# A layer norm's square root moved from all 128 partitions to four: Sqrt and reciprocal of per-token rows instead of Ln and Exp of a whole tile

## The reference

```python
def _layernorm(x, axis=-1, eps=1e-05):
    m = jnp.mean(x, axis=axis, keepdims=True)
    v = jnp.var(x, axis=axis, keepdims=True)
    return (x - m) / jnp.sqrt(v + eps)

x = L0_attn_x
x = x + 0.5 * _L0_ffn_ref(_layernorm(x, axis=-1), ...)     # two layers of local attention + GLU, each with a norm inside
x = x + _L0_attn_ref(_layernorm(x, axis=-1), ...)          # a scan
x = x + 0.5 * _L0_ffn_ref(_layernorm(x, axis=-1), ...)
x = x + 0.5 * _L1_ffn_ref(_layernorm(x, axis=-1), ...)     # spiking FFN
x = x + _L1_attn_ref(_layernorm(x, axis=-1), ...)          # 16 small heads
x = x + 0.5 * _L1_ffn_ref(_layernorm(x, axis=-1), ...)
x = x + 0.5 * _L2_ffn_ref(_layernorm(x, axis=-1), ...)
x = x + _L2_attn_ref(_layernorm(x, axis=-1), ...)
x = x + 0.5 * _L2_ffn_ref(_layernorm(x, axis=-1), ...)
x = x + 0.5 * _L3_ffn_ref(_layernorm(x, axis=-1), ...)     # 16 small heads, then routed experts, a norm before each
x = x + _L3_attn_ref(_layernorm(x, axis=-1), ...)          # a gated scan
x = x + 0.5 * _L3_ffn_ref(_layernorm(x, axis=-1), ...)
```

## Time and profile before

| what | value |
|---|---|
| median of 3 runs (lowest, highest) | 2577.56 us (2577.18, 2582.08) |
| the profiled execution, its own time | 2577.56 us |
| its span, first to last instruction | 2575.8 us |
| TensorE, matmuls | 1936.9 us, 75% |
| VectorE | 1377.8 us, 53% |
| ScalarE | 1184.5 us, 46% |
| GpSimd | 543.0 us, 21% |
| chain that ended last, by engine | PE 59%, DVE 19%, ACT 10%, issue 6% |

### The profile page before, as it was taken

The page is one execution under the profiler, slowest core; times in us unless marked ns, Lnnn a source line. Parts: engine busy times, 40 slices in busy tenths (PEclk is TensorE's granted clock), DMA queues, the critical chain, the costliest instruction groups (busy, mean ns, idle before and its releaser), DMA issues.

```text
span 2575.8 us, 36677 instructions
## 1 busy us (share of the span) xinstructions
PE 1936.9 (75%) x14096; PEld 962.2 (37%) x14096; DVE 1377.8 (53%) x2359; ACT 1184.5 (46%) x2408; POOL 543.0 (21%) x679
## 2 busy tenths in 40 slices
PE   6786877777787777868689964557898855688985
PEld 2444244433244423443234422223344442244434
DVE  4553465433555345543644367753677544467745
ACT  3454344432444425544524453235477724357762
POOL 2331134200333114320032000001322120223202
PEclk9998999988999799988879987688799977679997
DMA  3000000000000000000043000000444120243402
GB/s 138 1 2 1 0 1 1 2 0 0 1 1 1 1 0 1 1 1 1 0 97 60 3 0 0 0 0 20 97 86 88 26 66 0 49 88 79 86 16 82
DMA packets 50148, 70.81 MB, mean 27 GB/s; under 512 B 4980, under 2 KB 37972, under 8 KB 49464
## 3 DMA queue, kind: packets, MB, share of 16 engines
q1 hardware_dynamic: 47416, 60.07, 10.8%
q0 software_dynamic: 2560, 8.39, 1.2%
HBM read 50.59 MB, written 16.88 MB: 26 GB/s over the span
## 4 chain that ended last, share of the span: by engine, by line
PE 59%; DVE 19%; ACT 10%; issue 6%; POOL 4%; DMA 2%; SPq 0%; POOLq 0%; DVEq 0%; ACTq 0%
PE ps L196 56%; DVE arena L1144 3%; DVE arena L562 3%; ACT arena L509 2%; ACT arena L268 2%; ACT arena L270 2%; PE ps L425 2%; POOL arena L664 1%; POOL arena L657 1%; PE ps L1027 1%; DVE arena L635 1%; ACT arena L518 1%; DVE arena L908 1%; DVE arena L910 1%; DMA arena<-scratch 1%
## 5 line engine op out<-in xcount | busy, mean ns | idle before, releaser
L196 PE MATMUL ps<-arena 128*18 128x256 f32 (+10 forms) x10088 | 719.3, 313 | 196.2 <-DVE arena L1144 47.0
L196 PEld LDWEIGHTS ps<-arena 128*18 128x18 f32 (+6 forms) x10088 | 388.5, 127 | 509.8 <-issue 179.9
L1144 DVE TENSOR_REDUCE arena<-ps 128x2 f32<-128x512 f32 (+1 forms) x640 | 396.9, 661 | 239.2 <-PE ps L196 236.5
L196 PE MATMUL ps<-arena,w_L0f 128*128 128x512 f32 (+3 forms) x800 | 345.9, 569 | 95.9 <-DVE arena L573 28.3
L1128 ACT ACTIVATE arena<-ps 128x1024 f32<-128x1024 f32 (+1 forms) x320 | 313.1, 982 | 134.0 <-PE ps L196 129.6
L509 ACT ACTIVATE arena<-ps,arena 128x128 f32<-128x128 f32 x512 | 227.4, 459 | 112.0 <-DVE arena L606 111.9
L196 PE MATMUL ps<-arena,const 128*32 128x512 f32 (+2 forms) x616 | 228.8, 633 | 44.9 <-ACT arena L1467 19.5
L196 PEld LDWEIGHTS ps<-arena,w_L0f 128*128 128x128 f32 (+2 forms) x800 | 148.0, 201 | 257.2 <-issue 155.5
L664 POOL TENSOR_TENSOR arena<-arena 128x512 f32<-128x512 f32 x128 | 133.0, 1039 | 310.6 <-DVE arena L578 310.6
L562 DVE TENSOR_TENSOR arena<-ps,arena 128x1024 f32<-128x1024 f32 x128 | 152.7, 1220 | 66.8 <-PE ps L196 35.3
L518 ACT ACTIVATE arena<-ps 128x512 f32<-128x512 f32 x128 | 76.0, 598 | 226.2 <-PE ps L196 226.2
(11 more groups left out here) (227 smaller groups left out, 2286.7 us busy)
## 6 DMA issues: line engine op xcount, KB each, us to landing
scratch<-arena SPq DMA_DIRECT2D x40, 384.0 KB, 2.8
arena<-scratch SPq DMA_DIRECT2D x80, 192.0 KB
arena<-scratch SPq DMA_DIRECT2D x80, 128.0 KB
arena<-scratch SPq DMA_DIRECT2D x80, 88.0 KB
w_L0f<-in_L0f SPq DMA_DIRECT2D x2, 1557.0 KB, 12.2
arena<-arena SPq DMA_DIRECT2D x80, 12.0 KB
const<-in_const SPq DMA_DIRECT2D x1, 1276.0 KB, 7.6
residual<-in_x SPq DMA_DIRECT2D x1, 1024.0 KB, 5.0
```

The lines of the kernel that those rows point to most:

```text
L196: return self.nc.tensor.matmul(o, lhsT, rhs, start=start, stop=stop, skip_group_check=True)
L1144: V.tensor_reduce(self.mx[k % 2][:, :, at:at + 1], ps[:, i % 2, 0:SEQ + self.n1].rearrange("p (t s) -> p t s", t=self.blocks), AXX, ALU.ma ...
```

## The change

Each token's variance is now kept once instead of 128 times. For chunk c TensorE multiplies `sq` by `meanrow`, in four pieces of 128 tokens, so that row t of a 4x128 block holds the variances of piece t (in bank 2c+1, `k.tilerow` and `meanrow` exist already). ScalarE takes Sqrt of 4x128, VectorE its reciprocal, and TensorE spreads the four rows back to 128 partitions with `tilerow` (into the same bank). As a multiply would otherwise read two banks, ScalarE also copies x - m to the destination right behind the Square, and VectorE multiplies in place. Every step now runs over all four chunks before the next step begins, on each engine. The load at the start of a normalisation is gone.

```diff
 class Norm(Stage):
     def __init__(self, k, src, dst, eps, sq, sd, scale=None, shift=None):
...
-        self.logged, self.inverted = self.sig("logged", NCHUNK), self.sig("inverted", NCHUNK)
+        self.copied = self.sig("copied", NCHUNK)
+        self.rooted, self.inverted, self.spread = self.sig("rooted", NCHUNK), self.sig("inverted", NCHUNK), self.sig("spread", NCHUNK)
...
     def tensor(self, eng, src_ready=None):
         k, ps = self.k, self.k.ps
-        for c in range(NCHUNK + 1):
-            if c < NCHUNK:
-                if src_ready is not None:
-                    src_ready(eng, c)
-                k.mm(ps[:, 2 * c, :], k.K("center"), self.src[:, chunk(c)]).then_inc(self.centered.sem, 1)
-            if c > 0:
-                self.wait_ge(eng, self.squared, c)
-                k.mm(ps[:, 2 * c - 1, :], k.K("mean"), self.sq[:, chunk(c - 1)]).then_inc(self.summed.sem, 1)
+        for c in range(NCHUNK):
+            if src_ready is not None:
+                src_ready(eng, c)
+            k.mm(ps[:, 2 * c, :], k.K("center"), self.src[:, chunk(c)]).then_inc(self.centered.sem, 1)
+        for c in range(NCHUNK):
+            self.wait_ge(eng, self.squared, c + 1)
+            for t in range(4):
+                m = k.mm(ps[0:4, 2 * c + 1, 0:P], k.K("meanrow")[:, 4 * t:4 * t + 4],
+                         self.sq[:, c * CHUNK + t * P:c * CHUNK + (t + 1) * P], start=t == 0, stop=t == 3)
+            m.then_inc(self.summed.sem, 1)
+        for c in range(NCHUNK):
+            self.wait_ge(eng, self.inverted, c + 1)
+            for t in range(4):
+                m = k.mm(ps[:, 2 * c + 1, t * P:(t + 1) * P], k.tilerow[:, t * P:(t + 1) * P], self.sd[0:4, c * P:(c + 1) * P])
+            m.then_inc(self.spread.sem, 1)
 
     def scalar(self, eng):
         k, ps, S = self.k, self.k.ps, self.k.nc.scalar
-        S.preload_act_table_set("natural_log_exp_and_others")
-        for c in range(NCHUNK + 1):
-            if c < NCHUNK:
-                self.wait_ge(eng, self.centered, c + 1)
-                S.activation(self.sq[:, chunk(c)], ps[:, 2 * c, :], ACT.Square).then_inc(self.squared.sem, 1)
-            if c > 0:
-                sd = self.sd[:, chunk(c - 1)]
-                self.wait_ge(eng, self.summed, c)
-                S.activation(sd, ps[:, 2 * c - 1, :], ACT.Ln, bias=k.C(self.eps)).then_inc(self.logged.sem, 1)
-                self.wait_ge(eng, self.logged, c)
-                S.activation(sd, sd, ACT.Exp, scale=-0.5).then_inc(self.inverted.sem, 1)
+        for c in range(NCHUNK):
+            self.wait_ge(eng, self.centered, c + 1)
+            S.activation(self.sq[:, chunk(c)], ps[:, 2 * c, :], ACT.Square).then_inc(self.squared.sem, 1)
+            S.activation(self.dst[:, chunk(c)], ps[:, 2 * c, :], ACT.Copy).then_inc(self.copied.sem, 1)
+        for c in range(NCHUNK):
+            self.wait_ge(eng, self.summed, c + 1)
+            S.activation(self.sd[0:4, c * P:(c + 1) * P], ps[0:4, 2 * c + 1, 0:P], ACT.Sqrt, bias=k.C(self.eps)[0:4, :]).then_inc(self.rooted.sem, 1)
 
     def vector(self, eng, ch):
         k, ps, V = self.k, self.k.ps, self.k.nc.vector
         for c in range(NCHUNK):
-            self.wait_ge(eng, self.inverted, c + 1)
+            self.wait_ge(eng, self.rooted, c + 1)
+            r4 = self.sd[0:4, c * P:(c + 1) * P]
+            V.reciprocal(r4, r4).then_inc(self.inverted.sem, 1)
+        for c in range(NCHUNK):
+            self.wait_ge(eng, self.spread, c + 1)
+            self.wait_ge(eng, self.copied, c + 1)
             d = self.dst[:, chunk(c)]
-            if self.scale is None:
-                h = V.tensor_tensor(d, ps[:, 2 * c, :], self.sd[:, chunk(c)], ALU.mult)
-            else:
-                ch.did(V.scalar_tensor_tensor(d, ps[:, 2 * c, :], k.C(self.scale), self.sd[:, chunk(c)], ALU.mult, ALU.mult))
-                ch.wait_ge()
-                h = V.tensor_scalar(d, d, k.C(self.shift), None, ALU.add)
+            h = V.tensor_tensor(d, d, ps[:, 2 * c + 1, :], ALU.mult)
+            if self.scale is not None:
+                ch.did(h)
+                ch.wait_ge()
+                h = V.tensor_scalar(d, d, k.C(self.scale), k.C(self.shift), ALU.mult, ALU.add)
             h.then_inc(self.done.sem, 1)
```

## The result

| | time |
|---|---|
| before, median of 4 runs (lowest, highest) | 2577.43 us (2577.18, 2582.08) |
| after, median of 4 runs (lowest, highest) | 2661.99 us (2650.30, 2668.25) |
| ratio, 95% interval | 1.0336 (1.0303 to 1.0369) |
| forecast | 2653.5 us, range 2632 to 2690 |

The change makes the kernel 3.4% slower; the forecast had 2.95%. The profiled execution of after took 2663.19 us against 2577.56, 85.6 more. The chain of the new norm was forecast. That the sum came out near is partly luck: a norm that holds the clock costs less than I had (48 to 59 for 76, experiment 5), and a clock that does not hold, which I had left out, costs 27 to 39.

The account below looks back on a forecast made before the run. The prediction took ScalarE, at 1.72 us per chunk, to set the normalisation's pace. Its terms 12.9+8.7+18.3+13.0+10.8+12.2 = 75.9 us, added to 2577.6, gave 2653.5 us, range 2632 to 2690.

Parts of the forecast that it names:

- 76: All 20 normalisations and the stages they delay: the terms together add 75.9 us to the kernel's time.
- ScalarE's 1.72 per chunk: In the old normalisation, Square, Ln and Exp take 1.72 us per chunk, and ScalarE sets the pace.
- The reciprocals: On VectorE, four 4x128 reciprocals per normalisation, all ahead of the first multiply, 0.87 us each back to back.
- The loads: 13 square-root table loads between last Copy and first Sqrt, 1.28 us each; the other 7 normalisations need none.
- Rival 4: Each mid-normalisation load costs a second load length because ScalarE's queue must empty: +17, 2671 us; chance 0.03.
- cold, plain, with load: Normalisation starting at TensorE half clock, unscaled, with a Sqrt table load: last multiply ends at 14.9 us.
- warm, with load: Normalisation with TensorE at 2.4 GHz from the start and a Sqrt table load: ends at 13.05 us.
- two in a row, warm, and cold: Paired normalisations: the second's centring waits behind the first's spreads; ends 24.9 and 28.4 us, 12.2 more together.
- rival 1: Narrow passes of 4 columns or rows leave TensorE at 1.2 GHz, next stage starting at half clock: 2686 us; chance 0.12.
- two wide products of two passes each (4x0.43): Glu's start at chunk 1, at 14.75 us: these products put the first Gelu at 16.8 against 12.03.
- rival 3: TensorE stays awake through the normalisation, so following stages run at 2.4 GHz: 2564 us at 180 us; chance 0.02.
- Rival 2: In seven Glu, Scan and Spike starts, later work takes up the late normalisation: minus 31.3, 2622 us; chance 0.07.

Follow-up runs that it names:

- experiment 5: The changed kernel with the spreading passes over all 128 rows, zeros in the added ones; 2630.08 us, ratio 1.0186 to the kernel before.
- experiment 12: The kernel before with four extra 128-column passes on TensorE ahead of each of the 80 averaging passes; 2636.96 us, ratio 1.0245.
- Experiment 1: The changed kernel with each 4x128 reciprocal run twice on VectorE; 2733.33 us, ratio 1.0618 to the kernel before.
- experiment 3: The changed kernel with Ln and Exp on the four rows replacing Sqrt and reciprocal, their table loaded at the norm's start; 2641.91 us, ratio 1.0277.
- experiment 2: The changed kernel with the Sqrt table loaded at each norm's start instead of between Copy and Sqrt; 2646.19 us, ratio 1.0285.
- experiment 6: The kernel before, unchanged, timed against itself; 2569.19 us, ratio 0.998.
- experiment 10: The changed kernel with Ln and Exp on four rows, table loaded at the start, Copy moved to VectorE, spreading over 128 rows; 2621.07 us, ratio 1.0200.
- experiment 11: The kernel of experiment 10 with the spreading passes taking the four rows alone; 2649.46 us, ratio 1.0318 to the kernel before.
- experiment 9: The kernel of experiment 5 with 7 more Sqrt table loads behind the last Copy, 20 in all; 2626.39 us, ratio 1.0206 to the kernel before.

## Why the prediction was right, and where not

**The bound.** I read ScalarE's 1.72 per chunk as what sets the pace. It was half of the truth: TensorE's work per chunk is as long (experiment 12). That step failed without harm, since I priced the new norm by its own chain, in which TensorE appears.

**The reciprocals: right.** Forecast 0.87 back to back from the row of 0.940: 3.38 for four. It is the 128 along a partition that count. Experiment 1 shows that a further reciprocal lengthens the path; experiment 3, that TensorE's passes stand ready to set the end without them.

**The loads: right.** 13 of them, 0.01 to 0.02 between neighbours. Rival 4 is out: no load costs more than itself (13x1.28 = 16.6, and experiment 2 gave 13 to 16). The Trainium skill ("ScalarE: Activation LUTs", section "What ACT_TABLE_LOAD costs") has about 1380 ns of drain beside the 1283; none of the 13 shows it (17 to 19 ns before, 12 behind).

**The norm's end, from the first centring pass:**

| kind | forecast | measured |
|---|---|---|
| cold, plain, with load | 14.9 | 14.24 (second Spike); 16.25 (first L0Norm), 16.43 (first of the cold pair) |
| cold, no load (first L2Ffn) | 13.9 | 14.07 |
| warm, with load | 13.05 | 12.67 (last L2Ffn); 13.85 (L3Scan) |
| warm, no load | 11.8 | 11.78 (first of the warm pair); 12.65 (L2Attend) |
| scaled, with load | 17.1 | 16.67 |
| first Gelu | 16.8 | 17.61 |
| two in a row, warm, and cold | 24.9, 28.4 | 25.98, 30.96 |

Where a row has more than one value, the later ones are norms in which the clock fell during the spreads and stretched them (32 in 4.71 to 5.20 instead of 3.83); that is part of rival 1's picture, in 5 of 20 norms. In the two plain ones over 16 the centring passes also stayed longer at half clock (6.52 and 6.69, where I had 5.2).

**The terms of the sum**, by stage, against what the stages grew by (from the end of the stage before to their own end):

| stages | forecast | measured |
|---|---|---|
| L0Norm, L1Attend, L2Attend, L3Scan (5) | 12.9 | 11.7 |
| L2Ffn (2) | 8.7 | 8.7 |
| Glu (4) | 18.3 | 23.4 |
| Spike, Scan (3) | 13.0 | 14.2 |
| L3Experts (2) | 10.8 | 7.8 |
| L3Attend with two norms (2) | 12.2 | 12.0 |
| Attend behind L0Norm and Glu (4) | 0 | 7.0 |
| all | 75.9 | 84.9 of 85.6 |

The row of Glu fails most. Its step, "two wide products of two passes each (4x0.43)", takes full clock; these four passes ran from 557.47 to 560.91, 3.44 for 1.72, at half clock. They started 14.17 after the first centring pass where I had 14.75, which is why the first Gelu came only 0.8 late. Within the first row the single stages differ more (first L0Norm 5.1 for 3.4, L3Scan 6.1 for 3.1, L2Attend -2.2 for 1.9); those with Attend in them, the 7.0 of the last row too, are as uncertain as experiment 6 shows.

**Rival 1, held at 0.12, was half right.** "Passes with 4 columns or 4 rows": passes of four columns keep the clock up (in the Glu norm it stands at 1.0 through all sums), those of four rows don't. The clock did not stay low, as the rival had it; it was up and fell. The price I gave it was 32. Measured: 39 by the ratios of experiment 5, with an uncertainty of some 12, 28 in experiments 10 and 11, 27 by the spans of two single executions (2661.4 against 2634.3). **And the forecast's 76 was too high for a norm that holds the clock:** the span of experiment 5 is 58.6 above before, its median 48 by the ratio. Clock held, Glu grows by 4.1 to 4.3 instead of 4.4 to 4.75, the pairs' stages by 1.1 and 3.7 instead of 5.7 and 6.5, probably because the stage behind starts with the clock up: a piece of rival 3 (17 us for it at most, the whole difference). Two errors of opposite sign: by the spans 27 - 17 = 10, which is the 85.6 against the forecast's 75.9. Without the four Attend stages, L1Attend and L2Attend, where up to 6.1 came and went without any change in experiment 6, the picture is the same: forecast 71.9, after 79.5, experiment 5 57.2. So the sum lay in its range by luck as well as by reasoning: the term for the clock was left out, and the terms of the norms were together some 15 us too large.

**Rival 2** (the stage takes up the delay) is out: Glu, Spike and Scan grew by 4.1 to 6.6 each.

**Where the 84 us lie, then.** 27 to 39 are the clock that the four-row passes let fall. The rest, about 48 by experiment 5's ratio, is covered by TensorE's 32 spreading instructions a norm, which have no counterpart in before: as many passes alone cost 61 (experiment 12). Reciprocals, Copy and load lie beside this work and end a little later than it: with the clock held, taking the reciprocals and the middle load away and moving the Copy to VectorE, experiments 9 to 10, gives 5 us, which the intervals don't tell from nothing. What stays open: how the 48 and the 61 go together exactly (the averages of before are also replaced by sums of about the same length), and whether the early load is still worth something once the clock holds.

No kernel here beats the one before; the best with folded rows, experiments 5, 9 and 10, are 1.9 to 2.1% slower, and their intervals don't tell them apart.

## What to carry to other kernels

Before moving work off the engine that seems to set the pace, add up what each other engine does in the same stretch: here ScalarE and TensorE both filled 1.72 per chunk, so relief for ScalarE that was paid for in passes on TensorE could only lose. A cost found by doubling an instruction is what one more costs; what is gained by taking it out has to be tried by itself (71 against 4). And an operand of a few rows makes a pass neither shorter nor harmless: here it took as long as one over 128 rows, and the granted clock fell at it or behind it.

## What the runs showed of the hardware

- At a norm's 32 passes over four rows, or within 1.7 us behind them, the granted clock fell to half in 135 of 140 norms, also where TensorE had been busy for 3.80 of 3.80 us; with the same passes over 128 rows, zeros in the added ones, in 0 of 60. The Trainium skill ("TensorE: Matmul & The Clock Gate", section "What's actually happening") puts the gate down to how busy TensorE has recently been. By the profile's busy share both kernels are equally busy, so that rule alone does not tell them apart; the measurement decides. At the 32 passes of four columns over 128 rows the clock stayed at 1.00 in 20 of 20 norms of after.
- A pass over four rows and one over 128 follow each other at the same 0.11 us (32 in 3.83 and in 3.84).
- Over 21 runs of after (2650.3 to 2677.0) the time goes with the mean granted clock (correlation -0.98): each microsecond more at half clock goes with 0.29 us more. The profiled run of after has 655 us at half clock ((1 - 0.877) x 2 x 2663), that of experiment 5 has 580; by this slope, an estimate, 22 of the 27 us between their spans are the clock's.
